# One scale for all expert outputs and one sum for the first combine tile in a soft-MoE kernel

## The chip, the cores and the metric

The kernel runs on one core of one Trainium2 chip. Time is device time in microseconds (us), the median of the runs shown. A lower time is better. The engines are TensorE (PE in the profile; PEld is its weight load), VectorE (DVE), ScalarE (ACT), GpSimd (POOL) and SyncE (SP), which here issues nearly all DMAs.

## What is computed

Two layers, each with a residual around it. The first is linear attention and is not touched by the change. The second is a soft mixture of experts: `x` is 2 x 2048 x 256, read as `B=2` batches; there are 64 experts of 32 slots, so 2048 slots.

```python
# layer 1: x = x + LN(x_ln + proj(attention without softmax of x_ln))
# layer 2, of LN(x):
logits = einsum('bmd,dnp->bmnp', x, phi)
dispatch = softmax(logits, axis=0)                       # over the 2 batches
combine = softmax(logits.reshape(b, m, n*p), axis=-1)    # over the 2048 slots
slots = einsum('bmd,bmnp->bnpd', x, dispatch)
y = einsum('bnpd,nde->bnpe', slots, W) + b[None,:,None,:]
out = einsum('bnpd,bmnp->bmd', y, combine)
# x = x + LN(out)
```

## The kernel before

The program has three stretches: the first layer (to about 108 us), the **blocks** (to about 370 us) and the **combine** (to the end).

The 2048 slots are 16 expert tiles `t` of 128 slots (4 experts), in 4 blocks `nb` of 4 tiles. A block runs over 16 token tiles `j`. With two batches the dispatch softmax is a tanh of half the difference of the logits. So for each `j` TensorE makes the difference (`d_tile`, line 1576), ScalarE the tanh (`tanh`, 758) and a copy that is stored to memory (`d_copy`), VectorE splits the tanh into a high and a low half-precision part (`split`, 1117 and 1119), and TensorE adds the token tile into the slot sums (`slots`, 1589). The order on TensorE is slots(j), d_tile(j+2), slots(j+1). After j = 1, 5, 9, 13 it also multiplies a tile of slots of the block before with its experts' weights (`y_product`, 1606); VectorE adds the bias (`y_bias`, 1222) and ScalarE takes the largest absolute value (`y_sum`, 815). Weights come through two buffers `Wt`. A third, `Wx`, and a fourth, `Wz`, hold the weights of tiles 14 and 15, needed after the last block (`y_product3`, 1824).

Expert outputs `y` are used as a scaled high part `yh` and low part `yl` in half precision. `y_hi` (ScalarE, 828) makes the high part of a lot of 4 tiles of one batch, `y_lo` (VectorE, 1237 and 1241) the low part. Tiles 0 to 7 use one power-of-two scale, from the largest of their outputs (`top_of(0)`, `top_scale(0)` in the last block). Tiles 8 to 15 have a scale of their own, which can be made only when the last output exists, so `top_of(1)`, `top_scale(1)` and all four lots stand behind the last block. Their two lots of batch 0 have the low part made on GpSimd (lines 626 and 632).

In the combine, for each token tile `j`, TensorE makes the logits of batch 0 (`next_logits`, 1708, 96 matmuls; batch 1 follows by adding the stored difference), VectorE takes maxima (`l_max`, 1278), masks them (`mask1`, `mask0`, 1282), adds the difference (`add_max`, 1297), and makes the exponent's bias (`exp_bias`, 1303 and 1305) from a maximum that TensorE has spread over the partitions (`fold`, 1678). ScalarE takes the exponentials (`expo`, 868), VectorE transposes them (`turn`, 1262), ScalarE copies a high half (`hi`), VectorE or GpSimd (`lo` 1254, `lo_second` 581) makes the low half, and `combine(b, j)` on TensorE adds 16 tiles of three products: `high` (1726 and 1727) and `low` (1730). Batch 1 comes first, then batch 0. `u_copy`, `u_square`, `mean` and `finish` are the layer norm of the result and its store. The names `E1_ready`, `m0_masked`, `el_ready` and so on are semaphores: every engine's queue is written out by hand in its own block and runs strictly in order. Semaphores alone tie the queues together.

Since tiles 0 to 7 and 8 to 15 have different scales, token tile 0 is made as two sums in two PSUM banks (`first_combine`). `first_u_copy` rescales the first (by `rho`), `first_tail` adds the second, and then rescales `yh0` and the low parts of tiles 0 to 7 so that from token tile 1 on one sum does. SyncE loads for tile `j` the tokens (`load_x1`) and the stored difference (`load_d`) behind one wait.

Of the kernel before, what the change touches and what calls it, by code (L numbers as in the profile page):

```python
# [20 lines left out]
F16 = mybir.dt.float16  # L21
# [6 lines left out]
P = 128  # L28
# [63 lines left out]
def build(nc, x, norm_w, norm_b, qkv_w, qkv_b, proj_wT, proj_b, phi, ffn_w, ffn_bT, out):  # L92
# [24 lines left out]
    with ExitStack() as ctx:  # L117
# [37 lines left out]
        yhl1 = r_xn[:, 4096:8208].bitcast(F16).rearrange("p (b t c) -> p b t c", b=B, t=NT // 2)  # L155
# [53 lines left out]
        yabs3 = a.take(2048).rearrange("p (w n) -> p w n", w=4)  # L209
        ys = yabs3.rearrange("p w n -> p (w n)").rearrange("p (i t c) -> p i t c", i=2, c=C)  # L210
# [11 lines left out]
        def per_token():  # L222
# [8 lines left out]
        pm = sm.take(3)  # L231
# [4 lines left out]
        rho = sm.take(1)  # L236
# [54 lines left out]
        W2_loaded, W3_loaded, b23_loaded = sem("W2_loaded"), sem("W3_loaded"), sem("b23_loaded")  # L291
        ysum_ready, scale_ready, all_scales = sem("ysum_ready"), sem("scale_ready"), sem("all_scales")
# [5 lines left out]
        usum_ready = sem("usum_ready")  # L298
        el1_pool, yl_pool, stats_read = sem("el1_pool"), sem("yl_pool"), sem("stats_read")
# [10 lines left out]
        comb_done, ys_ready = sem("comb_done"), sem("ys_ready")  # L310
        yA_scaled = [sem(f"yA_scaled{b}") for b in range(B)]
        uA_copied, uB_added, u_copied, mean_ready, usq_ready = (
            sem("uA_copied"), sem("uB_added"), sem("u_copied"), sem("mean_ready"), sem("usq_ready"))
# [4 lines left out]
        y_lots = [(b, 2 * g + h) for g in range(2) for b in (1, 0) for h in range(2)]  # L318
# [32 lines left out]
        def _(sp):  # L351
# [29 lines left out]
            sp.dma_start(Wx, w_v[NT - 2]).then_inc(W2_loaded, 16)  # L381
# [8 lines left out]
            def block_io(nb, last):  # L390
                for j in range(NJ):
# [63 lines left out]
        def _(pool):  # L455
# [119 lines left out]
            pool.wait_ge(slots_used, NB * NJ + 2)  # L575
            nc.gpsimd.memset(yhl1[:, :, :, C:C + 1], 1.0).then_inc(zcol_ready, 1)  # L576
# [50 lines left out]
            own.wait()  # L627
            for i in range(2):
                pool.wait_ge(yh_ready, 7 + i)
                if i:  # L630
                    pool.wait_ge(ys_ready, 1)
# [3 lines left out]
            mean(1, 0)  # L635
            lo_second(1)
            mean(0, 1)
            finish(1, 0, 0, 0)
            finish(0, 0, 1, 0)
# [6 lines left out]
            with pool.Fori(1, NJ - 2) as j:  # L646
                own.enter(j - 1, 10)
                comb_pool(j)
                lo_second(j + 1)
                finish(0, j, 2 * j + 1, j)  # L650
                own.leave(NJ - 3)
# [7 lines left out]
        def _(act):  # L659
# [158 lines left out]
            def y_hi(i):  # L818

                b, h = y_lots[i]  # L820
                g = i // 4
                if g == 0:
                    act.wait_ge(scale_ready, 1)
                    out, scale = yh0[:, b, 4 * h:4 * h + 4, 0:C], sg[:, 1:2]
                else:
                    act.wait_ge(scale_ready, 2)
                    out, scale = yhl1[:, b, 4 * h - 8:4 * h - 4, 0:C], sg[:, 2:3]
                nc.scalar.activation(out, yf[:, b, 4 * h:4 * h + 4, :], ACT.Identity, scale=scale).then_inc(yh_ready, 1)

            def block_act(nb, last):  # L830
                for j in range(NJ):
                    tanh(nb, j)
                    d_copy(nb, j)
                    if j % 4 == 2:
# [5 lines left out]
                    if last and j in (5, 7, 9, 11):  # L840
                        y_hi((j - 5) // 2)

# [74 lines left out]
            def first_u_copy(b):  # L917
                act.wait_ge(comb_done, 2 - b)
                act.wait_ge(all_scales, 1)
                copy(u[:, 1 - b, :], bk[3 - b][:, 0:C], scale=rho).then_inc(uA_copied, 1)  # L920

            def first_u_sum(b):
                w = 1 - b
                act.wait_ge(uB_added, 2 - b)
                nc.scalar.activation(ujunk[:, w, :], u[:, w, :], ACT.Copy, accum_out=tl[:, w, 0:1]).then_inc(usum_ready, 1)
                eps_square(b, tl[:, w, 4:5], u_copied)

            def y_sum3(q):

                act.wait_ge(yp_done, (NB - 1) * TB + 2)  # L930
                y_sum((NB - 1) * TB + q, q, yabs3[:, q].rearrange("p (b c) -> p b c", b=B), ysum_ready)

# [953 lines left out]
```

## Time and profile before

| | us |
|---|---|
| median of 3 runs | 654.11 |
| lowest, highest | 654.04, 654.64 |
| the profiled execution | 654.63 |
| its span | 652.4 |

The profile is of one execution; 2.2 us of its time lie outside the span that the trace covers. Rows of the trace give a start in us from the span's start, a duration, the engine and the line of the kernel; in brackets stands the idle time before an instruction and what ended it. Matmul ends are modelled and overlap the next start, so for TensorE the starts count.

### The profile page before, as it was taken

The page shows a single profiled execution, that of the slowest core. Times are in us where ns is not written, and L with a number is a line of the kernel's source. Part 1 is how long each engine was busy: PE and PEld are TensorE (multiplying, and loading weights), DVE is VectorE, ACT ScalarE, POOL GpSimd, SP SyncE. Part 2 cuts the span into 40 slices and gives each one's busy share as a digit, 9 for nine tenths or more (in the row PEclk, how much of TensorE's full clock was granted, in tenths as well). Part 3 has the DMA queues.
Part 4 walks back from the last instruction along what each step waited for, and adds up shares of the span by engine and source line. Part 5 has one row for each costly group of instructions (what it writes and reads, how often), then busy time and mean ns, then how long its engine had stood idle before and what let it go on. Part 6 is the DMA issues. An engine that isn't in the chain of part 4 may idle for free.

```text
span 652.4 us, 15309 instructions
## 1 busy us (share of the span) xinstructions
PE 630.5 (97%) x5353; PEld 395.8 (61%) x5353; DVE 437.7 (67%) x859; ACT 367.3 (56%) x712; POOL 237.5 (36%) x416
## 2 busy tenths in 40 slices
PE   8999999999999999999999987799999999999996
PEld 7898645445444444444444455577777777777775
DVE  4978898733333423234333588999999988888885
ACT  5666876742333323324345295777777777777773
POOL 5365887710000000000000052555555555555555
PEclk9999999999999999999999999999999999999999
DMA  8910032325544544454455521132222222222201
GB/s 270 400 61 1 9 70 49 66 61 154 137 133 127 137 133 128 133 133 118 104 161 132 155 74 65 41 127 92 91 92 90 89 88 88 88 88 88 88 16 34
DMA packets 70167, 68.72 MB, mean 105 GB/s; under 512 B 6258, under 2 KB 66675, under 8 KB 67827
## 3 DMA queue, kind: packets, MB, share of 16 engines
q1 hardware_dynamic: 67792, 66.09, 34.4%
q10 hardware_dynamic: 2338, 2.16, 0.9%
q8 instruction: 21, 0.34, 0.2%
q14 instruction: 16, 0.12, 0.1%
HBM read 43.32 MB, written 23.07 MB: 102 GB/s over the span
## 4 chain that ended last, share of the span: by engine, by line
PE 75%; DVE 10%; POOL 5%; ACT 5%; issue 4%; DMA 1%; POOLq 0%; SPq 0%; DVEq 0%; ACTq 0%
PE psL L1589 23%; PE psM L1576 11%; PE psL L1708 10%; PE psM L1726 7%; PE psM L1727 6%; PE psM L1730 6%; PE psM L1606 3%; POOL small L489 2%; PE psL L1474 2%; ACT r_xn L868 1%; DVE small L1278 1%; DVE r_xn L1297 1%; ACT r L868 1%; DMA xres<-in_x 1%; PE psM L1532 1%
## 5 line engine op out<-in xcount | busy, mean ns | idle before, releaser
L1589 PE MATMUL psL<-r,r_xn 128*128 128x512 f16 x768 | 176.4, 379 | 0.8 <-DVE r L1119 0.8
L1589 PEld LDWEIGHTS psL<-r,r_xn 128*128 128x128 f16 x768 | 73.3, 98 | 91.6 <-issue 6.8
L1117 DVE TENSOR_SCALAR r<-r 128x512 f16<-128x512 f32 x64 | 29.0, 453 | 96.3 <-ACT r L758 96.3
L1576 PE MATMUL psM<-phs,xx 128*128 128x512 f16 (+1 forms) x384 | 93.2, 379 | 0.0
L758 ACT ACTIVATE r<-psM,small 128x512 f32<-128x512 f32 x64 | 43.6, 682 | 75.9 <-PE psM L1576 75.1
L576 POOL MEMSET r_xn<- 128x16 f16 x1 | 0.2, 173 | 234.9 <-PE psL L1589 234.9
L1708 PE MATMUL psL<-phs,r 128*32 128x512 f16 x1344 | 75.1, 379 | 2.0 <-DMA r<-xx 1.5
L1576 PEld LDWEIGHTS psM<-phs,xx 128*128 128x128 f16 x384 | 37.3, 98 | 44.8 <-issue 0.7
L868 ACT ACTIVATE r<-psL,small 128x512 f32<-128x512 f32 x60 | 41.9, 776 | 31.3 <-DVE small L1305 22.0
L489 POOL TENSOR_TENSOR small<-small,epst 128x2 f32<-128x2 f32 (+3 forms) x75 | 56.9, 759 | 6.2
L1708 PEld LDWEIGHTS psL<-phs,r 128*32 128x32 f16 x1344 | 34.6, 97 | 38.3 <-issue 2.6
L868 ACT ACTIVATE r_xn<-r_xn,small 128x512 f32<-128x512 f32 x64 | 47.1, 804 | 10.4 <-DVE small L1305 10.4
L815 ACT ACTIVATE r<-r_y 128x512 f32 (+1 forms) x16 | 10.0, 631 | 69.7 <-DVE r_y L1222 69.7
L594 POOL TENSOR_SCALAR small<-small 128x1 f32<-128x1 f32 x30 | 20.0, 666 | 76.1 <-ACT r L903 76.1
L1119 DVE SCALAR_TENSOR_TENSOR r<-r 128x512 f16<-128x512 f32 x64 | 45.2, 706 | 2.2
L1262 DVE STREAM_TRANSPOSE xx<-r_xn 128x1024 f32<-128x1024 f32 x32 | 39.8, 1245 | 9.4 <-ACT r_xn L868 8.5
L1222 DVE TENSOR_TENSOR r_y<-psM,r 128x512 f32 (+1 forms) x12 | 8.3, 692 | 51.4 <-PE psM L1606 51.4
L667 ACT ACTIVATE r<-psM 128x512 f32<-128x512 f32 (+1 forms) x67 | 39.1, 585 | 4.0 <-PE psM L1632 3.2
L1297 DVE CUSTOM_DVE_ANT_0 r_xn<-psL,xx 128x512 f32<-128x512 f32 x60 | 38.8, 685 | 2.4 <-issue 2.4
L1262 DVE STREAM_TRANSPOSE r<-r 128x1024 f32<-128x1024 f32 x32 | 39.6, 1239 | 0.4 <-ACT r L868 0.4
L1278 DVE TENSOR_REDUCE small<-psL 128x1 f32<-128x512 f32 x60 | 37.2, 683 | 0.0
L1254 DVE TENSOR_TENSOR r_xn<-r,r_xn 128x1024 f16<-128x1024 f32 x30 | 34.8, 1198 | 0.0
(208 smaller groups left out, 1292.7 us busy)
## 6 DMA issues: line engine op xcount, KB each, us to landing
logit_difference<-r SPq DMA_DIRECT2D x256, 64.0 KB, 1.8
xx<-logit_difference SPq DMA_DIRECT2D x16, 1024.0 KB, 5.2
r<-in_ffn_w SPq DMA_DIRECT2D x15, 1024.0 KB, 5.5
out<-r SPq DMA_DIRECT2D x32, 128.0 KB, 1.7
xres<-in_x SPq DMA_DIRECT2D x7, 512.0 KB, 11.0
r<-in_phi SPq DMA_DIRECT2D x1, 2048.0 KB, 18.1
expert_bias<-r ACTq DMA_DIRECT2D x1, 2048.0 KB, 20.0
r<-expert_bias SPq DMA_DIRECT2D x16, 128.0 KB, 2.2
```

What stands on the lines that cost most here:

```text
L489: return nc.gpsimd.tensor_tensor(o, v, epst[:, 0:1].broadcast_to([P, n]), ALU.pow)
L758: nc.scalar.activation(tF[:, j % 2, :], bk[j % 2][:, :], ACT.Tanh, scale=khalf).then_inc(t_ready, 1)
L868: nc.scalar.activation(E[b][:, c], src[:, c], ACT.Exp, bias=ebias[:, w, g:g + 1], scale=kap[:, 0:1]).then_inc(E_ready[b], 1)
L1119: V.scalar_tensor_tensor(thl[:, j % 2, 1], tF[:, j % 2], S_SCALE, thl[:, j % 2, 0], ALU.mult, ALU.subtract).then_inc(s_split, 1)
L1262: V.transpose(ET[b].rearrange("p (t g r) -> p g t r", g=GJ, r=Q)[:, g2], E[b].rearrange("p (g t c) -> p g t c", g=GJ, c=Q)[:, g2]).then_in ...
L1278: own.add(V.tensor_reduce(lmax[:, 0, g:g + 1], logits_at(j)[:, 512 * g:512 * g + 512], AX_X, ALU.max))
L1297: V.tensor_tensor_reduce(E0[:, c], logits_at(j)[:, c], dB[:, c], 1.0, -3.0e38, ALU.add, ALU.max, lmax[:, 1, g:g + 1]).then_inc(l_added, 1)
L1576: ins = mm(bk[j % 2][:, :].rearrange("p (q m) -> p q m", q=EP), xxT[:, 1, j, hx, k, :], phw[:, hp, k, :, bass.ds(nb, 1), :].rearrange("p q ...
L1589: ins = mm(psL[:, i * 512:(i + 1) * 512], x3n[:, b, j, hx, k * P:(k + 1) * P], thl[:, j % 2, hs, :], start=(j == 0 and hx + hs == 0), stop ...
L1708: ins = mm(logits_at(j)[q * Q:(q + 1) * Q, g * 512:(g + 1) * 512], xj[:, hx, k, g * Q:(g + 1) * Q], phs[:, hp, k, q * 512:(q + 1) * 512], ...
L1726: mm(acc, eT[b][:, 0, t, :], yh(b, t), start=first, stop=False)
L1727: mm(acc[:, 0:C], eT[b][:, 0, t, :], yl(b, t), start=False, stop=False)
```

## The change

- **Scale.** One power-of-two scale for all 16 tiles. It is made in the last block from the largest output of tiles 0 to 7 as before, and for tiles 8 to 15 from a bound: the largest entry of their weights times `T*C` (2048 x 256), and the largest bias `bmx` (one reduction in the first layer). For that the weights of tiles 7 to 14 are loaded a second time, into `Wx`, one after each fourth token tile of two blocks, and VectorE reduces 9 tiles of weights (`weight_max`) at j = 1, 5, 9, 13 of those blocks and at j = 1 of the last. `Wx` first holds tile 15, at the end tile 14 as before.
- **Gone:** the second `top_of`, `top_fold` and `top_scale`, `all_scale`, the `y_sum` of the last block and of the last four tiles, GpSimd's part of the low halves, `first_combine`, `first_u_copy`, `first_u_sum`, `first_tail` and the rescaling copy on ScalarE.
- **Moved:** the lots (b, h) = (1, 2) and (0, 2), tiles 8 to 11, have their `y_hi` at the end of the last block and their `y_lo` between the first `l_max`. For it `yhl1` is laid out by tile, so that its first half overlies tokens already used. The lots of tiles 12 to 15 stay behind it, both `y_lo` on VectorE.
- **First combine:** `combine(1, 0)` and `combine(0, 0)` are one sum each in one bank, with waits on the lots in the middle. Token tiles 1 and 2 are in the general loop on every engine. For tile 1 the mask is made by four VectorE instructions with a scalar (`mask_parts`) in place of one with two tensors.
- **Loads:** `load_x1(j)` waits only for the logits of the tile before, no longer for `m0_masked`.

```diff
@@ SyncE, block_io
+                    if j % 4 == 3 and not last:
+                        sp.wait_ge(W_max, (nb - 1) * TB + (q + 1))
+                        sp.dma_start(Wx, w_v[bass.ds((nb - 1) * TB + (q + NT // 2 - 1), 1)].rearrange(
+                            "t p n k e -> p (t n) k e")).then_inc(W2_loaded, 16)
@@ SyncE, loads
+                wait_apart(sp, l_done, 4 * j)
+                load_x1(j)
                 wait_apart(sp, m0_masked, j)
-                load_x1(j)
                 load_d(j)
@@ GpSimd
-            pool.wait_ge(scale_ready, 2)
-            pool.wait_ge(ysum_ready, 2 + NB * TB)
-            own.add(nc.gpsimd.tensor_scalar(ys[:, 0], yf[:, 0, 8:12, :], sg[:, 2:3], 0.0, ALU.mult, ALU.add))
...
-                nc.gpsimd.tensor_tensor(yhl1[:, 0, 4 * i:4 * i + 4, YC:YC + C], ys[:, i], yhl1[:, 0, 4 * i:4 * i + 4, 0:C],
-                                        ALU.subtract).then_inc(yl_pool, 1)
             lo_second(0)
@@ ScalarE, after the last block
             exps(1, 0, True)
-            y_sum3(0)
-            y_sum3(1)
-            y_sum3(2)
             act.wait_ge(m0_ready, 1)
-            expo(0, 0, 0)
-            expo(0, 0, 1)
-            y_sum3(3)
+            for g in range(GJ):
+                expo(0, 0, g)
+            y_hi(6)
             hi(1, 0, 0)
             hi(1, 0, 1)
-            expo(0, 0, 2)
-            expo(0, 0, 3)
-            y_hi(4)
-            y_hi(5)
+            y_hi(7)
             hi(0, 0, 0)
-            y_hi(6)
             hi(0, 0, 1)
...
+            act.wait_ge(all_scales, 1)
+            with act.Fori(1, NJ) as j:
                 comb_act(j)
@@ VectorE
+            def weight_max(i):
+
+                wait_apart(dve, W2_loaded, 16 * i + 16)
+                V.tensor_reduce(wmx[:, bass.ds(i, 1)], Wx.rearrange("p n k e -> p (n k e)"), AX_X, ALU.max,
+                                apply_absolute_value=True).then_inc(W_max, 1)
...
+                    if j % 4 == 1 and not last:
+                        weight_max((nb - 1) * TB + j // 4)
                     if last and j == 1:
-                        top_of(0)
+                        weight_max((NB - 2) * TB)
+                        top_of()
...
+            def comb_dve(j, first=False):
+                for g in range(GJ):
+                    l_max(j, g)
+                if first:
+                    mask_parts()
+                else:
                     mask1()
                 dve.wait_ge(ET_ready[0], 2 * j)
                 wait_apart(dve, dB_loaded, 16 * j + 16)
...
+                exp_bias(0, j, FOLD[1], m1_folded, m1_ready)
+                if first:
+                    y_lo(7)
                 add_max(j, 2)
                 add_max(j, 3)
                 mask0(j)
...
+            y_lo(6)
             comb_dve(1, True)
@@ TensorE, combine
+                    if first and t in (0, 8, 12):
+                        pe.wait_ge(yl_ready, {0: 4, 8: 6, 12: 8 - b}[t])
...
+            combine(1, 0, 0, True, True)
+            combine(0, 0, 1, True, True)
+            with pe.Fori(1, NJ - 1) as j:
                 next_logits(j + 1)
```

Where work moves, VectorE's queue shows it. First, the start of the last block, from `split(1)` to behind `y_bias` of the kernel before:

```order
L1117 TENSOR_SCALAR r<-r 128x512
L1119 SCALAR_TENSOR_TENSOR r<-r 128x512
L1192 TENSOR_REDUCE small<-small 128x1
L1194 STREAM_TRANSPOSE small<-small 128x32
L1196 TENSOR_REDUCE small<-small 128x1
L1198 TENSOR_SCALAR small<-small 128x4
L1117 TENSOR_SCALAR r<-r 128x512
L1119 SCALAR_TENSOR_TENSOR r<-r 128x512
L1222 TENSOR_TENSOR r_y<-psM,r 128x2x256
L1117 TENSOR_SCALAR r<-r 128x512
```

The same place with the change, where 1068 and 1070 are `split`, 1146 is `weight_max` and 1152 to 1164 are `top_of`:

```order
L1068 TENSOR_SCALAR r<-r 128x512
L1070 SCALAR_TENSOR_TENSOR r<-r 128x512
L1146 TENSOR_REDUCE small<-r 128x1
L1152 TENSOR_REDUCE small<-small 128x1
L1154 TENSOR_REDUCE small<-small 128x1
L1156 TENSOR_TENSOR small<-small 128x1
L1158 SCALAR_TENSOR_TENSOR small<-small 128x1
L1160 STREAM_TRANSPOSE small<-small 128x32
L1162 TENSOR_REDUCE small<-small 128x1
L1164 TENSOR_SCALAR small<-small 128x4
L1068 TENSOR_SCALAR r<-r 128x512
L1070 SCALAR_TENSOR_TENSOR r<-r 128x512
```

The reduction of a weight tile and three more small instructions stand ahead of `split(2)`.

Second, VectorE behind the last block, from the first `turn` of batch 0 to the mask of token tile 1, of the kernel before (1203 to 1073 are `top_scale(1)`, 1348 and 1349 `all_scale`):

```order
L1262 STREAM_TRANSPOSE xx<-r_xn 128x2x16x32
L1203 TENSOR_REDUCE small<-psM 128x1
L1067 TENSOR_SCALAR small<-small 128x1
L1069 TENSOR_SCALAR small<-small 128x1
L1071 TENSOR_SCALAR small<-small 128x1
L1073 RECIPROCAL small<-small 128x1
L1262 STREAM_TRANSPOSE xx<-r_xn 128x2x16x32
L1241 SCALAR_TENSOR_TENSOR r_xn<-r_y,small,r_xn 128x4x256 x2
L1348 TENSOR_TENSOR small<-small 128x1
L1349 TENSOR_SCALAR small<-small 128x1
L1278 TENSOR_REDUCE small<-psL 128x1 x4
L1282 TENSOR_TENSOR small<-small 128x16
```

With the change, from the last `turn` of batch 1 (1230 is `turn`, 1209 `y_lo`, 1246 `l_max`, 1279 `mask_parts`, 1265 `add_max`, 1271 and 1273 `exp_bias`):

```order
L1230 STREAM_TRANSPOSE r<-r 128x2x16x32
L1230 STREAM_TRANSPOSE xx<-r_xn 128x2x16x32 x2
L1209 SCALAR_TENSOR_TENSOR r_xn<-r_y,small,r_xn 128x4x256
L1246 TENSOR_REDUCE small<-psL 128x1 x4
L1279 TENSOR_SCALAR small<-small 128x4 x4
L1265 ISA r_xn,small<-psL,xx 128x512
L1265 ISA small 128x1
L1265 ISA r_xn,small<-psL,xx 128x512
L1265 ISA small 128x1
L1271 TENSOR_REDUCE small<-psM 128x4
L1273 TENSOR_SCALAR small<-small 128x4
L1209 SCALAR_TENSOR_TENSOR r_xn<-r_y,small,r_xn 128x4x256
```

The small chain between the turns is gone, one `y_lo` stands ahead of `l_max`, and the last `y_lo` has gone behind `exp_bias`, where it waits for nobody but delays the second pair of `add_max`.

## Rows read from the trace of the kernel before

**Rows 1.** The page: an engine's busy time, share of the span, instructions.
```profile
PE 630.5 (97%) x5353; PEld 395.8 (61%) x5353; DVE 437.7 (67%) x859; ACT 367.3 (56%) x712; POOL 237.5 (36%) x416
```

**Rows 2.** Windows from logits to logits: length, busy PE PEld DVE ACT POOL, clock, DMA.
```profile
378.60:401.05 22.45, 17.73 (x202) 12.48 (x194) 19.91 (x34) 15.93 (x23) 13.27 (x6) 1.00 0.11 43
401.05:422.48 21.43, 17.03 (x196) 11.99 (x196) 19.80 (x38) 15.55 (x29) 9.36 (x16) 1.00 0.20 65
422.48:439.26 16.78, 16.57 (x197) 12.05 (x198) 15.70 (x26) 12.28 (x24) 8.91 (x15) 1.00 0.32 118
439.26:455.56 16.30, 16.30 (x197) 12.05 (x196) 15.17 (x25) 11.81 (x24) 8.90 (x15) 1.00 0.27 91
```

**Rows 3.** Timeline of TensorE: where the logits of token tile 3 start.
```profile
422.48 5.36 PE L1708 MATMUL psL<-phs,r 128*32 128x512 f16 x96 [1.53 <-DMA r<-xx]
```

**Rows 4.** Timeline of VectorE between the last block and the combine's loop.
```profile
379.63 1.24 DVE L1262 STREAM_TRANSPOSE r<-r 128x1024 f32<-128x1024 f32 x1
...
389.63 2.02 DVE L1348 TENSOR_TENSOR small<-small 128x1 f32<-128x1 f32 x1
...
394.13 1.88 DVE L1282 TENSOR_TENSOR small<-small 128x16 f32<-128x16 f32 x1
...
432.56 1.32 DVE L1305 TENSOR_SCALAR small<-small 128x4 f32<-128x4 f32 x1
```

**Rows 5.** Timeline of GpSimd in the same stretch.
```profile
388.82 2.81 POOL L632 TENSOR_TENSOR r_xn<-r,r_xn 128x1024 f16<-128x1024 f32 x1 [0.18 <-ACT r_xn L828]
...
393.86 2.12 POOL L581 TENSOR_TENSOR r<-xx,r 128x1024 f16<-128x1024 f32 x1
...
431.73 2.13 POOL L581 TENSOR_TENSOR r<-xx,r 128x1024 f16<-128x1024 f32 x1
```

**Rows 6.** Groups by line: busy us, mean ns of one, idle before.
```profile
L1237 DVE SCALAR_TENSOR_TENSOR r_y<-r_y,small,r 128x1024 f16<-128x1024 f32 x4 | 5.1, 1278 | 0.0
L1278 DVE TENSOR_REDUCE small<-psL 128x1 f32<-128x512 f32 x60 | 37.2, 683 | 0.0
L1297 DVE CUSTOM_DVE_ANT_0 r_xn<-psL,xx 128x512 f32<-128x512 f32 x60 | 38.8, 685 | 2.4 <-issue 2.4
L1254 DVE TENSOR_TENSOR r<-xx,r 128x1024 f16<-128x1024 f32 x17 | 21.3, 1253 | 0.4 <-ACT r L667 0.4
L868 ACT ACTIVATE r<-psL,small 128x512 f32<-128x512 f32 x60 | 41.9, 776 | 31.3 <-DVE small L1305 22.0 <-DVE small L1297 9.3
L1076 DVE TENSOR_REDUCE small<-r 128x1 f32<-128x4096 f32 x1 | 4.4, 4390 | 0.0
```

**Rows 7.** Timeline in block 2: stores of j = 7, `split(9)`, `split(10)`, `slots(10)`.
```profile
183.60 2.17 SPq L371 DMA_DIRECT2D logit_difference<-r  x4
...
189.59 0.69 DVE L1119 SCALAR_TENSOR_TENSOR r<-r 128x512 f16<-128x512 f32 x1
193.01 0.43 DVE L1117 TENSOR_SCALAR r<-r 128x512 f16<-128x512 f32 x1 [2.73 <-ACT r L758]
...
197.94 2.76 PE L1589 MATMUL psL<-r,r_xn 128*128 128x512 f16 x12
```

**Rows 8.** The page's DMA issues: KB each, median us to landing.
```profile
r<-in_ffn_w SPq DMA_DIRECT2D x15, 1024.0 KB, 5.5
...
xres<-in_x SPq DMA_DIRECT2D x7, 512.0 KB, 11.0
```

**Rows 9.** Timeline of TensorE in the last block: `turn_x1`, then `slots`, twice.
```profile
307.34 0.61 PE L1665 MATMUL psM<-small,r_xn 128*128 128x128 f16 x8
...
307.97 2.76 PE L1589 MATMUL psL<-r,r_xn 128*128 128x512 f16 x12
...
315.88 0.61 PE L1665 MATMUL psM<-small,r_xn 128*128 128x128 f16 x8
316.33 2.75 PE L1589 MATMUL psL<-r,r_xn 128*128 128x512 f16 x12
```

**Rows 10.** Timeline of VectorE in the first layer: its wait behind the reduction of `phi`.
```profile
37.59 0.42 DVE L1039 TENSOR_TENSOR r<-r,r_xn 32x256 f32<-32x256 f32 x1 [2.09 <-ACT r L667]
```

More of the change, by code:

```diff
@@ L230, in build @@
         ve = sm.take(48)
[L231 removed]
+        pm = sm.take(2)
+        wmx, wtop, bmx = sm.take(NT // 2 + 1), sm.take(1), sm.take(1)
         gm = sm.take(3)
@@ L833, in block_act @@
                     d_copy(nb, j)
-                    if j % 4 == 2:
+                    if j % 4 == 2 and not last:
                         q = j // 4
@@ L841, in block_act @@
                         y_hi((j - 5) // 2)
+                if last:
+                    y_hi(4)
+                    y_hi(5)
             with act.Fori(1, NB - 1) as nb:
@@ L1305, in exp_bias, with mask_parts @@
                 V.tensor_scalar(ebias[:, w], m1[:, w], kap[:, 1:2], E_LOG, ALU.mult, ALU.add).then_inc(done, 1)
-            def comb_dve(j, first, third=False):
-                if not first:
-                    for g in range(GJ):
-                        l_max(j, g)
+            def mask_parts():
+                own.wait()
+                for g in range(GJ):
+                    ins = V.tensor_scalar(fmax[:, 0, :, g], fmask[:, :, g], lmax[:, 0, g:g + 1], None, ALU.mult)
+                    if g < GJ - 1:
+                        own.add(ins)
+                ins.then_inc(m1_masked, 1)
+            def comb_dve(j, first=False):
+                for g in range(GJ):
+                    l_max(j, g)
+                if first:
+                    mask_parts()
+                else:
                     mask1()
@@ L1324, in comb_dve @@
                 mask0(j)
-                if first:
-                    first_tail(1)
-                elif not third:
-                    lo(0, j - 1, 0)
+                lo(0, j - 1, 0)
                 turns(1, j, first)
                 turn(1, j, 0)
-                exp_bias(1, j, FOLD[1 if first else 0], m0_folded, m0_ready)
+                exp_bias(1, j, FOLD[0], m0_folded, m0_ready)
                 turn(1, j, 1)
@@ L1383, in _ @@
             turn(1, 0, 1)
-            top_of(1)
             dve.wait_ge(yp_done, NB * TB)
             turn(0, 0, 0)
-            top_scale(1, bk[1][:, 304:304 + EP])
             turn(0, 0, 1)
-            y_lo(4)
-            y_lo(5)
-            all_scale()
-            l_max(1, 0)
-            l_max(1, 1)
-            l_max(1, 2)
-            l_max(1, 3)
-            mask1()
-            lo(0, 0, 0)
-            comb_dve(1, True)
-            comb_dve(2, False, True)
-            with dve.Fori(3, NJ) as j:
-                own.enter(j - 3, 6)
-                comb_dve(j, False)
-                own.leave(NJ - 3)
+            y_lo(6)
+            comb_dve(1, True)
+            with dve.Fori(2, NJ) as j:
+                own.enter(j - 2, 6)
+                comb_dve(j)
+                own.leave(NJ - 2)
             lo(0, NJ - 1, 0)
@@ L1783, in combine @@
                 pe.wait_ge(eh_ready[b], 2 * j + 1)
                 for t in range(NT):
+                    if first and t in (0, 8, 12):
+                        pe.wait_ge(yl_ready, {0: 4, 8: 6, 12: 8 - b}[t])
                     if t == 8:
-                        if second and not b:
-                            fold(0, j + 1, FOLD[1], m1_masked, m1_folded)
-                        elif more and not b:
+                        if more and not b and not first:
                             fold(1, j + 1, FOLD[0], m0_masked, m0_folded)
@@ L1791, in combine @@
                     high(b, t, acc, t == 0)
-                if b and more and not second:
-                    fold(0, j + 1, FOLD[1], m1_masked, m1_folded)
+                if more and (b or first):
+                    fold(1 - b, j + 1, FOLD[b], (m0_masked, m1_masked)[b], (m0_folded, m1_folded)[b])
                 for t in range(NT):
                     if t % 8 == 0:
-                        lows_ready(b, j, t // 8, not more)
+                        if first and b:
+                            pe.wait_ge(el1_pool, 1 + t // 8)
+                        else:
+                            lows_ready(b, j, t // 8, not more)
                     ins = low(b, t, acc, t == NT - 1)
```

208 lines of the change are left out of this document (52 added, 156 removed).

## The prediction, made before the changed kernel ran

> **What bounds the kernel now.** I read the page first: TensorE is busy for 97% of the span [rows 1], so time can only go where TensorE stands still or does less. The change leaves its matmuls as they are, but for one small `top_fold`. Next I cut the trace at the places where the logits of a token tile start [rows 2]. From 439.26 on the combine's loop takes 16.30 us a turn and TensorE is busy for all of it: that is the floor of a turn. The three turns before hold the same work (96 matmuls of logits and two `combine`s) and take 22.45, 21.43 and 16.78 us. Over the floor that is 6.15 + 5.13 + 0.48 = 11.76 us, the most that this stretch can give. The clock is 1.00, the full level of 2.4 GHz, in all four windows, so nothing of it is clock. VectorE is busy for 19.91 of 22.45 and 19.80 of 21.43 us there, against 15.17 in a turn of the loop [rows 2]: it is the engine that TensorE waits for.
>
> **The change: the first turn, 378.60 to 401.05.** What goes from VectorE is the chain of `top_of(1)`, `top_scale(1)` and `all_scale`, one rescaling, and two `y_lo` (moved). Part of their price is the lock with GpSimd that the rows show: the one-element L1348 took 2.02 us and ended at 391.65, when GpSimd's L632 ended (388.82 + 2.81 = 391.63), and L1282 took 1.88 us, until GpSimd's L581 ended (393.86 + 2.12 = 395.98) [rows 4, 5].
>
> VectorE's new queue from the end of the last `turn` of batch 1, 380.8 [rows 4], goes by durations of [rows 4, 6], where a `turn` costs 1.2, a pair of `add_max` 1.3 and `lo` 1.2: two turns to 383.2, `y_lo(6)` to 384.5, four `l_max` (0.62 apart) to 387.0, the four instructions of `mask_parts` to 387.4, `add_max` to 388.7, `exp_bias` 0.4. ScalarE feeds this in time: four `expo` of at most 0.78 us [rows 6] and the moved lots put `y_hi(6)` at 382.5 and its last `hi` at 387.4. GpSimd's three low halves of 2.1 us each [rows 5] follow those `hi`s, from 384.5 to about 390.9, because `y_lo(6)` holds the first one up. So `exp_bias` falls into the third. Its scalar instruction is of the kind that took 1.32 us against GpSimd's 431.73 + 2.13 [rows 4, 5], so I let it wait to 391.0, which is the bound from above; 389.1 is the bound from below. Then `y_lo(7)` to 392.3, `add_max` to 393.6, `mask0` to 393.8, `lo(0,0,0)` to 395.0. TensorE's own work from 378.60 would be done at 378.60 + 16.30 = 394.9, but its last 16 `low` matmuls, some 1.8 us, stand behind that `lo`: the logits of tile 2 start at 396.8. ScalarE's exponentials of tile 1, which held them in the kernel before, are then done at about 394.3. With the lower bound the turn ends at 395.0. I take 396.6, near the upper one, since the trace shows three such locks. First turn: 18.0 us in place of 22.45, so 4.45 gained.
>
> **The second and third turn.** Both `first_tail`s go (VectorE had 4.6 us more to do here than in the loop [rows 2]), and so do the rescalings and the second bank. The wait of 1.53 us for tokens [rows 3] goes with `load_x1`, now issued when the logits before are done, a turn ahead of need. What remains is the loop's body. VectorE comes into it some 1.4 us later than it does in the loop, where its masks lie about that much ahead of TensorE's `fold`s, and it has 16.30 - 15.17 = 1.1 us of room per turn. I take 16.5 and 16.3 us: 4.9 + 0.5 = 5.4 gained. Bounds: nothing left over the floor (5.6), or half of the second turn's excess left (3.0). What is late next is nothing that can be named: TensorE itself.
>
> **The blocks.** Added are 9 reductions of 2048 elements on VectorE. Half of L1076, which takes 4.39 us for 4096 [rows 6], is 2.2 us each, 20 us in all. None of it is on the path unless `split` of the next token tile comes late. `Wx` is issued behind the stores of j = 7, at about 185.9, and at 5.5 us [rows 7, 8] lands at 191.4. VectorE stands at that wait from 190.3, and queued behind it is `split(10)`, which could start at 193.0. It starts at 193.6 instead and ends at 194.8. TensorE wants it at 197.94 [rows 7], since `y_product` comes first: 3.1 us to spare. In the last block `weight_max` and the longer `top_of` (seven small instructions, about 1.5 us) are one behind the other, and about 2.3 us stay. On SyncE the load stands ahead of the stores of j = 8. Their 256 KB then land some 2 us later, but the buffer is wanted again only by `d_copy(10)`, and what that frees only by `d_tile(12)`, behind `slots(10)`. Cost: nothing. The two moved `y_lo` (1.28 each [rows 6]) fill the gaps between `l_max` while VectorE waits for logits, and the `y_hi` are in ScalarE's pause after its last `d_copy`. If that cover failed they would cost up to 2.6 us. The added reduction of the bias, about 0.35 us, ends in front of a wait of 2.09 us for ScalarE [rows 10]: nothing.
>
> **A small gain** in the last block: without `y_sum`, ScalarE's tanh of j = 3, 7 and 11 no longer waits for `y_bias`. `slots` then follows the turned tokens after 0.45 us, as at 315.88, and not after 0.63, as at 307.34 [rows 9]. Three times 0.18 is 0.5 us.
>
> **A rule against the change.** `mask_parts` replaces a mask that reads two tensors, and no row shows whether a strided scalar instruction of four elements is held by GpSimd. The Trainium skill ("SBUF — State Buffer", Who interferes with whom) says that the port pair shared by VectorE and GpSimd is held for a whole instruction, and counts `tensor_scalar` in its two-port modes among those that take it. L1305 at 1.32 us agrees.
>
> **Rivals.**
> - *All masks are locked too.* `mask_parts` waits for two of GpSimd's low halves, to 391.1, and everything behind comes 1.9 us later: the logits of tile 2 start at 398.5, and the gain is 2.55 + 5.4 + 0.5 = 8.5 us, 645.6. For it: the three locks of before. Against: the shape is another. By the skill's rule this is what happens.
> - *VectorE stays late.* It enters the loop 3 us behind, and the second turn keeps half its excess, the third all of it: 3.2 + 2.5 + 0 + 0.5 = 6.2, 647.9. For: VectorE has only 1.1 us of room a turn. Against: TensorE's queue itself starts later then.
> - *No lock bites,* everything goes: 11.76 + 0.5 = 12.2, 641.9.
> - *The weights come late: slower.* The 8 added loads share the queues with 64 KB stores. The first loads of the program took 11.0 us for 512 KB [rows 8]. TensorE stalls once a load takes over 5.5 + 3.1 = 8.6 us. At 9.9 us the eight stalls of 1.3 eat the gain. At 11.0 they cost 8 x 2.4 = 19 us, and the time is 654.1 + 19 - 10.3 = 663. For: VectorE's queue is strictly in order, so one late load stops `split`. Against: the loads now in that place take 5.5 us, and the DMA engines are half idle.
> - *It does not do what it says:* the late lots only move the wait. `combine(1, 0)` now waits for `y_hi(6)`, `y_hi(7)` and `y_lo(7)` inside one sum, and the gain stays within 1 us, 653.5. Against: by the queue above those lots are there before TensorE asks, by 0 to 2 us.
>
> **How the numbers follow.** 4.45 + 5.4 + 0.5 = 10.3 us against the profiled execution's 654.63 gives 644.3. That execution lies 0.5 above the median, so I forecast 643.8. Chances: forecast 0.50, masks locked 0.15, VectorE late 0.12, no lock 0.09, no gain 0.06, late weights 0.08. Leaving out the last two leaves 0.86 and the range 641.9 to 647.9. A measurement of this kernel can tell 0.2% (1.3 us) from no change: faster 0.86, same 0.06, slower 0.08.
>
> **What would show it.** In the new trace: the distances between the starts of the logits should be near 18.0, 16.5, 16.3. The scalar part of the first `exp_bias` behind `mask_parts` should be long (up to 2 us) if the lock is right; long `mask_parts` speak for the first rival. VectorE should stand for about 1 us ahead of each `weight_max`, of 2.2 us, with no idle TensorE between 150 and 370. Idle TensorE ahead of `slots(10)` would make the prediction wrong, and so would second and third turns above 17 us.

## The result, and the profile after

| | before | after |
|---|---|---|
| median | 654.38 | 646.32 |
| lowest, highest | 654.04, 655.03 | 646.22, 646.81 |
| the profiled execution | 654.63 | 646.24 |
| its span | 652.4 | 644.1 |

The ratio is 0.9877, with a 95% interval of 0.986 to 0.9894. The change gains 8.06 us where 10.3 were forecast: the sign and the places are right, and one term is too large. The windows from logits to logits of the changed kernel answer to [rows 2] (length, busy PE PEld DVE ACT POOL, granted clock, DMA share, GB/s):

```profile
377.57:398.94 21.37, 18.20 (x200) 13.11 (x192) 19.63 (x30) 13.25 (x19) 7.17 (x4) 0.92 0.24 87
398.94:415.21 16.27, 16.27 (x198) 12.03 (x197) 15.20 (x25) 11.75 (x23) 8.91 (x15) 1.00 0.21 74
415.21:431.48 16.27, 16.27 (x199) 12.04 (x198) 15.19 (x25) 11.78 (x24) 8.91 (x15) 1.00 0.25 95
431.48:447.75 16.27, 16.27 (x200) 12.03 (x199) 15.09 (x26) 11.78 (x24) 8.90 (x15) 1.00 0.26 90
```

The second and third turns, 21.43 and 16.78 us before, are at the floor: 5.16 + 0.51 = 5.67 gained, forecast 5.4. The first turn, forecast at 18.0, takes 21.37 in place of 22.45 and gives 1.08, forecast 4.45. The stretch ahead of it is 1.03 shorter (377.57 against 378.60), and what follows 431.48 is 0.5 shorter than what follows 439.26 before. That is 8.3, the difference of the spans.

In the first turn VectorE is still busy for 19.63 us, and the clock is 0.92: TensorE lost time in a way that no rival had. VectorE's timeline there (start, duration):

```profile
385.66 4.02 DVE L1279 TENSOR_SCALAR small<-small 128x4 f32<-128x4 f32 x4
...
391.01 0.23 DVE L1273 TENSOR_SCALAR small<-small 128x4 f32<-128x4 f32 x1
```

And GpSimd's:

```profile
382.41 4.90 POOL L624 TENSOR_TENSOR r_xn<-r,r_xn 128x1024 f16<-128x1024 f32 x2 [13.99 <-ACT r_xn L656]
387.26 2.12 POOL L584 TENSOR_TENSOR r<-xx,r 128x1024 f16<-128x1024 f32 x1
```

Line 1279 is `mask_parts`: four instructions on four elements each, taken as 0.4 us, took 4.02. The view of the line itself gives a shortest, a middle and a longest one:

```profile
L1279 DVE TENSOR_SCALAR small<-small x4: 220/948/2165, 385.7 to 389.5; 128x4 f32<-128x4 f32 x4
```

The first lasted until L624 ended (382.41 + 4.90 = 387.31), the second, of 2.17, until L584 ended (387.26 + 2.12 = 389.38), and the last two took 0.22 each, so the form by itself is not slow. `exp_bias` (L1273), which I had expected to be held, came after all that and took 0.23. What TensorE did with it:

```profile
389.73 0.40 PE L1617 MATMUL psM<-small,w_fold 128*128 128x16 f32 x2 [3.17 <-DVE small L1279]
389.98 1.34 PE L1669 MATMUL psM<-r,r_xn 128*128 128x257 f16 x8
391.11 1.93 PE L1669 MATMUL psM<-r_xn 128*128 128x257 f16 x8
```

Eight of its matmuls take 1.34 and 1.93 us where they take 1.05 elsewhere. Windows of one us, the clock being the number behind POOL's, show why:

```profile
389.00:390.00 1.00, 0.27 (x3) 0.27 (x4) 1.00 (x4) 0.00 (x0) 0.39 (x1) 1.00 0.00 0
390.00:391.00 1.00, 1.00 (x10) 0.82 (x10) 0.98 (x5) 0.00 (x0) 0.00 (x0) 0.80 0.00 0
391.00:392.00 1.00, 1.00 (x7) 0.68 (x6) 0.99 (x2) 0.64 (x1) 0.00 (x0) 0.50 0.00 0
392.00:393.00 1.00, 1.00 (x6) 0.72 (x5) 1.00 (x4) 0.81 (x2) 0.00 (x0) 0.50 0.00 0
393.00:394.00 1.00, 1.00 (x7) 0.70 (x5) 0.96 (x6) 0.93 (x2) 0.00 (x0) 0.50 0.00 0
394.00:395.00 1.00, 1.00 (x11) 0.89 (x10) 1.00 (x2) 1.00 (x4) 0.00 (x0) 0.99 0.51 66
```

Some 0.9 us after it had started again from its pause of 3.17 us, TensorE fell to 0.50, the level of 1.2 GHz, and stayed there from about 390.6 to 394.0: 6 or 7 matmuls start in a us, not 11.

The blocks are as forecast. VectorE's timeline at block 2, which answers to [rows 7]:

```profile
191.56 2.29 DVE L1146 TENSOR_REDUCE small<-r 128x2048 f32 x1 [1.76 <-DMA r<-in_ffn_w]
193.77 0.42 DVE L1068 TENSOR_SCALAR r<-r 128x512 f16<-128x512 f32 x1
```

`weight_max` waits 1.76 us for its weights, forecast 1.1, and takes 2.29, and `split(10)` starts at 193.77, forecast 193.6. `slots(10)` starts at 197.46 with no idle TensorE ahead of it, and none is seen in this trace between 110 and 370.

### The profile page after: what moved, and what is told of

Read it like the earlier page. It is cut to its first block, busy times and chain, and to the rows that moved or that the text cites. A ratio compares the mean times of both kernels' runs of the same rounds, so it can differ in the third digit from the quotient of the medians.

```text
span 644.1 us, 15376 instructions
## 1 busy us (share of the span) xinstructions
PE 628.2 (98%) x5351; PEld 395.3 (61%) x5351; DVE 454.1 (70%) x858; ACT 359.4 (56%) x692; POOL 231.2 (36%) x414
## 4 chain that ended last, share of the span: by engine, by line
PE 81%; DVE 6%; POOL 5%; issue 3%; ACT 2%; DMA 2%; SPq 1%; POOLq 0%; ACTq 0%; DVEq 0%
PE psL L1528 24%; PE psL L1647 12%; PE psM L1515 11%; PE psM L1665 8%; PE psM L1669 8%; PE psM L1666 8%; PE psM L1545 3%; POOL small L491 2%; DMA r_xn<-in_proj_wT 2%; PE psL L1733 1%; PE psL L1413 1%; PE psM L1471 1%; DVE phs L1049 1%; POOL r_xn L562 1%; PE psM L1617 1%
## 5 line engine op out<-in xcount | busy, mean ns | idle before, releaser
L895 ACT ACTIVATE r<-r,small 128x256 f32<-128x256 f32 x30 | 15.0, 500 | 34.4 <-POOL small L591 34.4
```

## Experiments

Theory: two things make the first turn longer than forecast. GpSimd holds up the four mask instructions, and the pause that this gives TensorE costs clock behind it. Rivals: VectorE would be late anyway; the added weight loads disturb; the clock fall is the whole of it.

**1. The masks in a form that may escape GpSimd**

```diff
-                for g in range(GJ):
-                    ins = V.tensor_scalar(fmax[:, 0, :, g], fmask[:, :, g], lmax[:, 0, g:g + 1], None, ALU.mult)
+                for q in range(EP):
+                    rows = slice(q * Q, (q + 1) * Q)
+                    ins = V.tensor_reduce(fmax[rows, 0, q, :], lmax[rows, 0, :].unsqueeze(2), AX_X, ALU.max)
```

> The changed kernel with the four mask_parts instructions (scalar instructions of four elements) replaced by four tensor_reduce over one quadrant each; the values are the same. Theory (GpSimd's lock): each scalar instruction stood at the port that GpSimd held, 385.66 to 389.68 in the trace of the changed kernel; a reduction of one input is not held, so the four take under 0.6 us together. TensorE's wait of 3.17 us ahead of the fold goes, and with it the fall of its clock. Behind it the exp_bias instruction is now held until GpSimd's third low half ends, about 389.4, so the first turn ends about 395.2 and not 398.9: 646.3 - 3.7 = 642.6 us, between 641.5 and 643.5. Rival (the four instructions are slow because of their scalar pointers and own semaphores): the four reductions take about 1 us each too and the time stays 646.3 +- 0.4.

Measured: 643.69 us (643.14 to 644.10), ratio 0.9829 (0.9813 to 0.9846). VectorE's timeline:

```profile
386.70 0.69 DVE L1280 TENSOR_REDUCE small<-small 32x4 f32<-32x4 f32 x4
...
388.85 1.61 DVE L1273 TENSOR_SCALAR small<-small 128x4 f32<-128x4 f32 x1
```

GpSimd's timeline beside it:

```profile
383.45 4.91 POOL L624 TENSOR_TENSOR r_xn<-r,r_xn 128x1024 f16<-128x1024 f32 x2 [13.99 <-ACT r_xn L656]
388.31 2.13 POOL L584 TENSOR_TENSOR r<-xx,r 128x1024 f16<-128x1024 f32 x1
```

All four reductions ran in 0.69 us in the middle of GpSimd's L624, so the theory holds for the masks: four instructions in a row are not slow for their semaphores. Then `exp_bias` was held for 1.61 us, until L584 ended at 388.31 + 2.13 = 390.44: just the step of my prediction. The logits start at 378.62, 396.15 and 413.13, so the turns are 17.53 and 16.98. TensorE's longest pause is 0.74 us and the mean clock of the execution 0.999. The time is 1.1 above what was expected and 0.2 outside its range: the turns keep 1.3 and 0.7 us over the floor.

**2. TensorE kept busy through the wait**

```diff
+                if first and b:
+                    for _ in range(28):
+                        mm(bk[0][:, 0:C], eT[1][:, 0, 0, :], yh(1, 0)[:, 0:C], start=True, stop=True)
                 if more and (b or first):
                     fold(1 - b, j + 1, FOLD[b], ...)
```

> The changed kernel with 28 more matmuls of 256 columns into an unused bank, in TensorE's queue ahead of the first fold of combine(1, 0), where it stood for 3.17 us; their results are not used. The lock stays. Theory (the fall of the clock has a price of its own): the granted clock stays 1.00 through 386 to 396 and the 3.2 us at half clock go back to 1.6, so the time is 646.3 - 1.6 = 644.7, between 644.2 and 645.3. Rival (the path is VectorE's and TensorE at half clock cost nothing): 646.3 +- 0.3 with the clock at 1.00.

Measured: 645.51 us (645.27 to 645.79), ratio 0.986 (0.9843 to 0.9876). The masks were held as before:

```profile
386.30 4.02 DVE L1279 TENSOR_SCALAR small<-small 128x4 f32<-128x4 f32 x4
```

The clock stayed at 1.00, and the logits at 378.22, 397.93 and 414.55 give turns of 19.71 and 16.62. The first turn is 1.66 shorter than in the changed kernel, the second 0.35 longer. The median gains 0.8 where 1.6 was expected: 0.2 outside the theory's range and 0.5 below the rival's. So the fall has a price, by the median half of the forecast one; 0.4 us of the rest is lost elsewhere in this trace (see experiment 3). That parts the two causes: full clock leaves the hold, and the hold is the larger part.

**3. Without the weights**

```diff
-                    if j % 4 == 3 and not last:
-                        sp.wait_ge(W_max, (nb - 1) * TB + (q + 1))
-                        sp.dma_start(Wx, ...)
...
-                    if j % 4 == 1 and not last:
-                        weight_max((nb - 1) * TB + j // 4)
...
-                        weight_max((NB - 2) * TB)
```

> The changed kernel without the 8 second loads of weights and the 9 weight_max; this leaves out the weights' part of the scale (only the largest of tiles 0 to 7 and of the bias counts). Theory (they lie wholly beside TensorE): 646.3 +- 0.3. Rival (they cost something, by late split or by the traffic): up to 9 x 0.3 = 2.7 us less, 643.6 to 645.8.

Measured: 646.17 us (645.59 to 647.51), ratio 0.9873 (0.9857 to 0.989). Eight loads of 1 MB and nine reductions less change the median by 0.15, with a spread of 1.9 us between the executions. (The scale then rests on tiles 0 to 7 and the bias alone, and `Wx` holds tile 14 from the start.) The cost of 0 that the prediction gave them holds to within that spread, and the rival's largest, 2.7 us, is out.

One place is less safe than it looks. This is `weight_max` at j = 1 of the last block in the changed kernel:

```profile
296.83 2.29 DVE L1146 TENSOR_REDUCE small<-r 128x1 f32<-128x2048 f32 x1 [1.35 <-DMA r<-in_ffn_w]
```

And in experiment 2, with `slots(2)` behind it:

```profile
298.89 2.29 DVE L1146 TENSOR_REDUCE small<-r 128x1 f32<-128x2048 f32 x1 [3.17 <-DMA r<-in_ffn_w]
...
303.61 2.76 PE L1528 MATMUL psL<-r,r_xn 128*128 128x512 f16 x12 [0.33 <-DVE r L1070]
```

In experiment 2 the reduction starts 8.4 us after the load was issued (290.54), in the changed kernel 6.5 us after it (290.29). `split(2)` came late behind it, and `slots(2)` follows `slots(1)` by 6.24 us in place of 5.84. In the trace of experiment 5 it is 6.01; in the other seven traces with these loads TensorE doesn't wait there. This is the rival of late weights at a small price, 0.4 us in one execution.

**4. One mask instruction with two tensors, as in the kernel before**

```diff
-                if first:
-                    mask_parts()
-                else:
-                    mask1()
+                mask1()
```

> The changed kernel with mask_parts undone: for token tile 1 the one instruction with two tensors, as for all other tiles. Theory (every instruction that meets GpSimd's lock is one chance to be held, and four in a row are held twice): the one instruction starts at 385.66, is held until the second low half ends at 387.3, 1.7 us, and the fold can start 2.3 us earlier than in the changed kernel. TensorE stands for 1 us and its clock stays full. The rest is then set by exp_bias, held until 389.4, as without any lock on the mask: 642.7 us, between 641.7 and 644.0. Rival (four small instructions without a second tensor are the better form): slower than 646.3 by up to 2 us.

Measured: 643.69 us (643.39 to 644.12), ratio 0.9832 (0.9816 to 0.9848). The mask in VectorE's timeline:

```profile
386.52 1.69 DVE L1250 TENSOR_TENSOR small<-small 128x16 f32<-128x16 f32 x1
...
389.55 0.74 DVE L1273 TENSOR_SCALAR small<-small 128x4 f32<-128x4 f32 x1
390.21 1.27 DVE L1209 SCALAR_TENSOR_TENSOR r_xn<-r_y,small,r_xn 128x1024 f16<-128x1024 f32 x1
```

The one instruction is held too, but once. It ends with L624, and `exp_bias` is held for some 0.5 us more. Windows of its first two turns:

```profile
378.44:395.98 17.54, 16.70 (x200) 12.33 (x193) 17.01 (x27) 12.47 (x18) 7.19 (x4) 1.00 0.23 83
395.98:412.95 16.97, 16.53 (x197) 12.02 (x196) 15.90 (x26) 12.45 (x24) 8.92 (x15) 1.00 0.26 94
```

17.54 + 16.97 = 34.51, against 21.37 + 16.27 = 37.64 in the changed kernel. So `mask_parts` costs 2.6 us of median by itself, the fall of the clock with it: between two of its instructions GpSimd's next one starts, and each that meets one waits for all of it.

**5. GpSimd's low half later** (on top of 4)

```diff
+            pool.wait_ge(yl_ready, 8)
             lo_second(0)
```

> The changed kernel with one mask instruction in place of mask_parts (as e4_mask_one, 643.69 us), and GpSimd's first low half of the combine waits until the last y_lo (tile 12 to 15, batch 1) is written. In e4 that half runs from 388.14 to 390.26, right behind GpSimd's other long pair, and VectorE does not stand there for more than 0.5 us. Theory A (the lock only moves): the half now starts at about 391.5 and ends at 393.6; the second mask, a TENSOR_TENSOR on small tiles, is held from 392.7 to 393.6 and lo follows at 393.7 in place of 392.8; TensorE's last low matmuls and the logits of tile 2 start 0.9 us later: 644.6 us (range 644.1 to 645.2), first turn 18.4. Theory B (the early half is what costs, as my prediction had it for exp_bias): first turn shorter than e4's 17.54 by 0.5 us or more and the time 643.2 or less.

Measured: 644.10 us (643.36 to 644.38), ratio 0.9839 (0.9822 to 0.9855). VectorE's timeline:

```profile
389.48 0.23 DVE L1274 TENSOR_SCALAR small<-small 128x4 f32<-128x4 f32 x1
...
392.15 0.99 DVE L1251 TENSOR_TENSOR small<-small 128x16 f32<-128x16 f32 x1
```

GpSimd's:

```profile
390.97 2.13 POOL L584 TENSOR_TENSOR r<-xx,r 128x1024 f16<-128x1024 f32 x1 [2.87 <-DVE r_xn L1210]
```

`exp_bias` is free now (0.23), and the second mask is held instead, until 390.97 + 2.13 = 393.10. Theory A: the hold moves with GpSimd's instruction. The first turn is 17.83, 0.3 longer than in 4; 18.4 was expected. The times lie at the lower end of what was expected and overlap those of 4 (643.39 to 644.12), so the rows show this and the medians do not.

**6. `y_lo` behind the mask** (on top of 4)

```diff
                 mask1()
+                if first:
+                    y_lo(6)
...
-            y_lo(6)
             comb_dve(1, True)
```

> The changed kernel with one mask instruction (as e4_mask_one, 643.69 us), and the y_lo ahead of the four l_max moved behind the mask. In e4 the y_lo took 1.24 us from 382.85, the maxima 384.01 to 386.49, and the mask was held from 386.52 until GpSimd's pair ended at 388.14. Now the maxima end at about 385.3 and the mask should be done at 385.9, when the first of GpSimd's two is over. Theory A (y_lo is then held by GpSimd's second instruction until 388.1): TensorE's last 8 high matmuls of combine(1, 0), wanted at 386.4, start at 388.1, the fold follows at 389.0 in place of 388.26: 644.4 us (range 643.9 to 645.0). Theory B (only small masks are held, a y_lo of 1024 elements is not): y_lo ends at 387.2, VectorE is 0.9 us earlier from there on, the first turn falls from 17.54 to about 17.3 and the second from 16.97 to 16.3: 642.9 us (range 642.5 to 643.4).

Measured: 645.17 us (644.89 to 645.53), ratio 0.9859 (0.9842 to 0.9875). VectorE's timeline:

```profile
384.77 0.18 DVE L1250 TENSOR_TENSOR small<-small 128x16 f32<-128x16 f32 x1
384.86 3.16 DVE L1209 SCALAR_TENSOR_TENSOR r_xn<-r_y,small,r_xn 128x1024 f16<-128x1024 f32 x1
```

GpSimd's:

```profile
382.71 4.23 POOL L624 TENSOR_TENSOR r_xn<-r,r_xn 128x1024 f16<-128x1024 f32 x2 [13.99 <-ACT r_xn L656]
386.90 3.11 POOL L584 TENSOR_TENSOR r<-xx,r 128x1024 f16<-128x1024 f32 x1
```

TensorE's:

```profile
388.08 0.28 PE L1663 MATMUL psM<-r_xn 128*128 128x257 f16 x1 [2.09 <-DVE r_xn L1209]
```

Theory A by its mechanism: the mask slips between GpSimd's two instructions (0.18), and the `y_lo`, 1.27 elsewhere, takes 3.16. It waits for the end of L624 at 386.94 and then runs for its 1.1 us, while L584 in its turn is held: 3.11 in place of 2.13. TensorE waits 2.09 us for it, more than the 1.7 expected, and its clock falls behind that pause too (0.66 from 388 to 389, 0.50 in the two us after). All four executions have a mean clock of 0.996, and the median is 0.8 above the expectation, 0.2 outside its range.

**7. `load_x1` late again**

```diff
-                wait_apart(sp, l_done, 4 * j)
-                load_x1(j)
                 wait_apart(sp, m0_masked, j)
+                load_x1(j)
                 load_d(j)
```

> The changed kernel with the load of tokens (load_x1) behind the wait for mask0 again, as in the kernel before. Theory A (the wait of 1.53 us in the kernel before came from a late mask, not from the place of the load): mask0 of the second turn is done at about 409.6, the load lands 2.1 to 2.6 us behind its issue at about 412.5, and the logits want it at 415.21: nothing is lost, 646.3 us (range 645.9 to 646.7), no idle TensorE ahead of the logits. Theory B (my prediction: the wait goes with the place of load_x1): a wait of about 1.5 us comes back, 647.8 us.

Measured: 645.62 us (644.93 to 646.86), ratio 0.9871 (0.9854 to 0.9887). Windows of the first two turns:

```profile
377.77:397.48 19.71, 16.54 (x201) 12.26 (x193) 19.17 (x30) 12.81 (x19) 7.17 (x4) 1.00 0.23 84
397.48:414.08 16.60, 16.53 (x198) 12.03 (x197) 15.53 (x26) 12.09 (x24) 8.90 (x15) 1.00 0.21 69
```

No wait for tokens came back. The load goes out at 410.35, and the logits want it at 414.08. The masks are held here as well and TensorE pauses for the same 3.17 us, but in this profiled execution the clock stayed at 1.00, and the first turn is 19.71, not 21.37. Two of the four executions, at 644.93 and 645.03, have a mean clock of 0.998 and more, which fits a median 0.3 below theory A's range. Theory B wanted 647.8.

**8. `load_x1` early in the kernel before**

```diff
+                wait_apart(sp, l_done, 4 * j)
+                load_x1(j)
                 wait_apart(sp, m0_masked, j)
-                load_x1(j)
                 load_d(j)
```

> The kernel before with only load_x1 moved ahead of the wait for mask0. Theory A (VectorE sets the end of the second turn, the wait for tokens lies over it): the wait of 1.53 us at 422.48 goes, but the third turn gets longer by as much, since VectorE is no earlier: 654.4 us (range 653.9 to 654.8). Theory B (the wait is on the path by itself): 654.6 - 1.5 = 653.1 us (range 652.9 to 653.5).

Measured: 654.48 us (654.22 to 655.19), ratio 1.0002 (0.9992 to 1.0011). Windows of its turns:

```profile
378.02:400.44 22.42, 18.47 (x203) 12.91 (x196) 19.90 (x34) 15.90 (x23) 13.27 (x6) 0.94 0.10 38
400.44:420.43 19.99, 18.59 (x197) 12.51 (x197) 18.13 (x35) 14.57 (x26) 8.49 (x14) 0.89 0.18 66
420.43:438.65 18.22, 16.83 (x196) 12.17 (x196) 17.10 (x29) 13.26 (x27) 9.79 (x17) 1.00 0.37 129
```

TensorE's timeline in the third:

```profile
430.39 0.39 PE L1679 MATMUL psM<-small,w_fold 128*128 128x16 f32 x2 [0.95 <-DVE small L1283]
434.76 0.40 PE L1679 MATMUL psM<-small,w_fold 128*128 128x16 f32 x2 [0.44 <-DVE small L1283]
```

Theory A. The second turn is 1.44 shorter than in [rows 2] and the third 1.44 longer; the wait for the load became waits for VectorE's masks. The clock fell here, to 0.94 and 0.89 in two windows, and no cost of it shows: the five executions with a mean clock of 0.996 or less have a median of 654.75, the five others one of 654.43, with a spread of 0.8 and 0.9 us.

**9. `y_sum` back in the last block**

```diff
-                    if j % 4 == 2 and not last:
+                    if j % 4 == 2:
```

(their result is not used)

> The changed kernel with y_sum back in the last block (three more ScalarE instructions there, at j = 2, 6, 10; their result is not used). Theory A (my prediction's small gain): slots follows the turned tokens after 0.63 in place of 0.45 us at j = 3, 7, 11 and the time is 646.3 + 0.5 = 646.8 us (range 646.6 to 647.1). Theory B (the 0.55 us that the last block gained come from elsewhere): no change, 646.3 us.

Measured: 647.01 us (645.83 to 647.40), ratio 0.9888 (0.9871 to 0.9904). TensorE's timeline at j = 3, where `slots` follows `turn_x1`:

```profile
307.18 0.61 PE L1604 MATMUL psM<-small,r_xn 128*128 128x128 f16 x8
307.80 0.39 PE L1528 MATMUL psL<-r,r_xn 128*128 128x512 f16 x1
```

The changed kernel at the same place, which answers to [rows 9]:

```profile
306.86 0.61 PE L1604 MATMUL psM<-small,r_xn 128*128 128x128 f16 x8
307.31 1.03 PE L1528 MATMUL psL<-r,r_xn 128*128 128x512 f16 x4
```

0.62 us with `y_sum`, 0.45 without, and so at the two other places. From `slots` of j = 1 to the first logits the trace shows 81.03 us here (297.44 to 378.47), 81.00 in the kernel before (297.60 to 378.60) and 80.45 in the changed one (297.12 to 377.57). The small gain of 0.55 is this. The median agrees (0.7), though the spread of executions is as large.

**10. The changed kernel once more**

> The changed kernel once more, unchanged. Two profiled executions with the same 3.17 us of idle TensorE ahead of the fold differ: in e6_x1_late and e8_ysum the clock stayed at 1.00 and the first turn took 19.7 us, in the first profile of this kernel and in e3_no_weights it fell to 0.50 for about 3 us and the turn took 21.4. Theory A (the fall comes in some executions only): the times spread over 1.0 us or more, with executions near 645.0 (mean clock 0.998 and up) and near 646.3 (0.996 to 0.997). Theory B (this kernel always has it, the variants have it less for another reason): all executions within 646.0 and 646.9.

Measured: 646.15 us (644.51 to 646.35), ratio 0.9867 (0.985 to 0.9883). Theory A. Three executions lie at 646.05, 646.25 and 646.35 with mean clocks of 0.996 to 0.997, one at 644.51 with 0.999. Experiment 7 had 644.93 and 645.03 (0.998, 0.999) beside 646.21 and 646.86 (0.996, 0.997). By the mean clocks the same program loses clock in most executions, 7 of its 8 here. Of the profiled executions with the pause of 3.17 us, three have the fall (the changed kernel, experiments 3 and 10) and two have not (7 and 9). Executions with and without it lie 1.6 us apart in experiment 7 and 1.7 in experiment 10.

## Why the prediction came out as it did

**What bounds the kernel** was read rightly. The masks that TensorE waits for, the logits-to-logits distances and the floor of a turn were the right places to look, and at the floor it is TensorE itself.

**The first turn** is the term that was mis-sized, and the step that failed is "the four instructions of `mask_parts` to 387.4", 0.4 us for four. They took 4.02. I had the rule, three rows of it, and a rival for it, and gave that rival 0.15 because "the shape is another". Its price was good: logits of tile 2 19.9 us behind those of tile 1. At full clock experiments 7 and 9 show 19.71 and 19.70, where I forecast 18.0. I should have taken the hold as the case and its absence as the rival, since the four instructions stand exactly where GpSimd has its long ones, and L1305, a scalar instruction of four elements, was among the rows as held. The Trainium skill ("SBUF — State Buffer", Who interferes with whom) counts `tensor_scalar` among the operations that can take the port pair shared with GpSimd, if their operands fit, and says that the engine that comes second is blocked for the whole instruction. The trace agrees with it: two of the four waited for the end of one GpSimd instruction each, 4.02 us in all.

**The clock** was in no term and no rival. In the kernel before, once its first 8 us are over, TensorE's longest pause is 1.58 us (ahead of 418.87), and the clock is 1.00. A pause of 3.17 us was new, and what it cost stands in the difference of the windows: 37.64 us for two turns with the fall, 19.71 + 16.60 = 36.31 without, that is 1.33. By medians it is 0.8 (experiment 2), by single executions 1.6 to 1.7 (7 and 10). A long pause is not all that can bring a fall: in experiment 8 none ahead of it was above 0.98 us. The Trainium skill ("TensorE: Matmul & The Clock Gate", Part 1) says that what watches TensorE's activity runs free of the kernel, so that the same kernel has a different number of slow matmuls at its start from run to run. That the fall behind a pause comes in some executions only would fit this; no run here can show that it is the reason.

**The sum.** With one mask instruction (experiment 4) the two turns take 34.51 us, and 18.0 + 16.5 = 34.5 was forecast. Its median of 643.69 stands beside the forecast of 643.8. So the forecast is about the kernel without `mask_parts`. That it fits so well is partly luck: the mask was held for 1.69, which I had left out, and `exp_bias` for 0.74 where I had put in 1.9. GpSimd's three low halves, forecast from 384.5 to 390.9, ran in the changed kernel from 382.41 to 389.38, so the place where they meet VectorE's queue was off by 1.5 us.

**Second and third turn:** 5.67 us against 5.4, right. But a part of it came as a gift: with the first turn at 21.37 VectorE comes in with time in hand, and both turns are at the floor. When the first turn is short (experiments 1 and 4) the second takes 16.97: VectorE enters late, and TensorE waits 0.45 us for a mask. Ahead of that mask stands one more hold, in experiment 4 this one, beside GpSimd's 405.44 + 2.13:

```profile
406.23 1.37 DVE L1273 TENSOR_SCALAR small<-small 128x4 f32<-128x4 f32 x1
```

The instruction takes 0.23 when free. The turns of the loop have this hold too, 1.32 us in the kernel before [rows 4], but there VectorE has the time for it. This is what "VectorE comes into it some 1.4 us later" meant, and I priced it at 0.2 where it is 0.7. It is also, with 0.7 us, most of why experiments 1 and 4 stayed 1 us above what I expected of them.

**The wait of 1.53 us for tokens** [rows 3]. "The wait goes with `load_x1`, now issued when the logits before are done" is wrong as a cause. It goes with the earlier masks: experiment 7 has the load behind the mask and no wait, experiment 8 has it early and no gain. The sum didn't suffer, since I took the turn to the floor as a whole.

**The blocks:** nothing in this trace, as forecast; the load and `split(10)` came within 0.2 us of the forecast, the wait for the weights was 1.76 and not 1.1, and experiment 3 takes them away with no effect that its spread would show. A load takes 5.7 us by the page (median of 23), 5.5 was assumed. The 2.3 us of cover in the last block were too few in two of nine traces (experiment 3). **The small gain** of 0.5 is 0.55 in the traces, by experiment 9.

**Left over:** 0.48 us were gained before `slots(10)` of block 2 (197.46 against 197.94), where the change does next to nothing. The start of the first logits differs between executions of kernels with the same work up to there by more than that (377.57, 377.63, 377.77, 378.62), so I put it down to that spread; it was not tested. The 0.5 behind 431.48 was in no term either. Of it, 0.44 is in the next eleven turns, 178.93 us in place of 179.37, so 16.27 each in place of 16.31. Experiment 8 has 16.31 too, all kernels with the change have 16.27. What in the change does it is open; a candidate that was not tried is the new layout of `yhl1`, which TensorE reads in each turn.

## What to carry to other kernels

Where two engines hold each other up by the instruction, count the starts that can meet the other engine's long instruction, not the elements. Splitting one tiny instruction into four beside GpSimd's long ones made 4.02 us of it, where the one took 1.69. Price such a place first from the rows of what is held, and look for a form of the instruction that isn't, or for a place between the other's instructions. A wait that names a late load is not proof that the load is late by itself: move it alone in the kernel before, as in experiment 8, and see where the time goes.

## What the runs showed of the hardware

- A `TENSOR_REDUCE` over 32 x 4 elements was not held by GpSimd (four in 0.69 us); `TENSOR_SCALAR` on 128 x 4, `TENSOR_TENSOR` on 128 x 16 and `SCALAR_TENSOR_TENSOR` on 128 x 1024 were, and took up to some 2 us longer for it. Whether the operation or the 32 partitions of the reductions made the difference was not tried.
- The hold works both ways: GpSimd's instruction of 2.13 us took 3.11 behind a held `y_lo` (experiment 6).
- TensorE's clock was at 0.50 for about 3.4 us behind pauses of 3.17 us (in 7 of 8 executions of the changed kernel, by their mean clocks) and 2.09 us (4 of 4). In experiment 8 it fell too, with no pause above 0.98 us ahead of it but VectorE setting the pace, and then the time was the same within the spread. Here a fall cost time only where the rest waited for TensorE.
